# Half-width score tiles, transposed initial states, four-bank spreads and the first groups' sums on VectorE, in a four-layer kernel

## The reference

```python
x = L0(ctx, x, mask)    # attention over concat(ctx, x): 16 heads of 16, 128 keys; RMS norm; gelu MLP; both + x
x = L1(x, state=ctx)    # RWKV-like block; 32 heads of 8; a recurrence over the 64 tokens:
    # s_new = k (x) v + w * s ;  out = r . (faaaa * k (x) v + s) ;  s0 = ctx[:, 2:10]; then a gated channel mix
x = L2(x, ctx, masks)   # causal-style self attention, cross attention to ctx (64 keys each), gelu MLP, layer norms
x = L3(x, ctx, mask)    # x + tanh(gate) * attention of x over layernorm(ctx), 64 keys
```

## Time and profile before

| | |
|---|---|
| median of 3 runs | 1057.02 us (1055.05 to 1059.72) |
| profiled execution, own time | 1057.86 us |
| its span, first to last instruction | 1056.1 us |
| PE busy | 998.5 us (95%) |
| PE weight loads busy | 805.9 us |
| DVE, ACT, POOL busy | 717.6, 599.9, 543.0 us |
| PE's mean granted clock | 0.969 of full |

### The profile page before, as it was taken

The page is one execution under the profiler, slowest core; times in us unless marked ns, Lnnn a source line. Parts: engine busy times, 40 slices in busy tenths (PEclk is TensorE's granted clock), DMA queues, the critical chain, the costliest instruction groups (busy, mean ns, idle before and its releaser), DMA issues.

```text
span 1056.1 us, 27681 instructions
## 1 busy us (share of the span) xinstructions
PE 998.5 (95%) x10976; PEld 805.9 (76%) x10976; DVE 717.6 (68%) x1575; ACT 599.9 (57%) x1460; POOL 543.0 (51%) x666
## 2 busy tenths in 40 slices
PE   7768999989999999999999999999999999999997
PEld 4556877667777778888788877767878778888886
DVE  1224236898899879597553536877899888874765
ACT  2469854324444465546887875227555554675672
POOL 0445325664566655467541436636556774664432
PEclk9958999899999999999999999999999999999999
DMA  9601110001000101001020100100010000000001
GB/s 345 249 2 27 26 25 1 2 2 25 2 2 2 33 2 33 2 24 46 12 58 13 37 2 1 48 1 2 1 27 1 2 13 2 13 2 13 13 2 43
DMA packets 28400, 30.47 MB, mean 29 GB/s; under 512 B 16560, under 2 KB 25072, under 8 KB 27632
## 3 DMA queue, kind: packets, MB, share of 16 engines
q1 hardware_dynamic: 27248, 26.85, 7.9%
q10 hardware_dynamic: 1024, 1.85, 0.5%
HBM read 26.59 MB, written 2.10 MB: 27 GB/s over the span
## 4 chain that ended last, share of the span: by engine, by line
PE 70%; DVE 10%; DVEq 5%; issue 5%; ACT 4%; POOL 3%; ACTq 1%; POOLq 1%; DMA 1%
PE bank L504 10%; PE bank L492 10%; PE bank L366 7%; PE bank L378 7%; PE bank L399 7%; PE bank L391 4%; PE bank L435 3%; PE bank L455 3%; PE bank L479 3%; PE bank L533 3%; PE bank L522 3%; DVE lane L1002 2%; DVEq L1005 2%; DVE bank L998 2%; PE bank L659 2%
## 5 line engine op out<-in xcount | busy, mean ns | idle before, releaser
L1403 POOL TENSOR_TENSOR lane<-lane 128x512 f32<-128x512 f32 x160 | 166.6, 1044 | 210.6 <-DVE lane L881 112.0
L1175 ACT COPY lane<-bank 128x512 f32<-128x512 f32 x232 | 131.3, 586 | 158.3 <-PE bank L366 91.7
L366 PE MATMUL bank<-ident,lane 128*128 128x128 f32 x896 | 136.0, 286 | 15.0 <-ACTq L1238 4.5
L366 PEld LDWEIGHTS bank<-ident,lane 128*128 128x128 f32 x896 | 105.8, 146 | 39.1 <-issue 14.9
L1472 POOL TENSOR_TENSOR lane<-lane 128x512 f32<-128x512 f32 x64 | 81.2, 1269 | 67.3 <-DVE lane L1002 66.9
L1236 ACT ACTIVATE lane<-bank,lane 128x128 f32<-128x128 f32 x256 | 90.7, 372 | 22.3 <-DVE lane L931 21.8
L879 DVE TENSOR_REDUCE lane<-lane 128x8 f32<-128x512 f32 x96 | 65.0, 677 | 30.1 <-ACT lane L1194 29.5
L1002 DVE TENSOR_TENSOR_SCAN lane<-lane,bank 128x256 f32<-128x256 f32 x128 | 80.9, 674 | 5.0 <-issue 0.4
L1143 ACT ACTIVATE lane<-lane 128x256 f32<-128x256 f32 x96 | 52.4, 594 | 49.9 <-POOL lane L1388 49.2
L1157 ACT ACTIVATE lane<-bank,vecs 128x256 f32<-128x256 f32 x112 | 55.7, 552 | 42.4 <-PE bank L366 42.1
L1194 ACT ACTIVATE lane<-lane 128x512 f32<-128x512 f32 x96 | 60.3, 634 | 19.7 <-DVE lane L861 19.4
(11 more groups left out here) (159 smaller groups left out, 2298.3 us busy)
## 6 DMA issues: line engine op xcount, KB each, us to landing
lane<-in_inT SPq DMA_DIRECT2D x16, 256.0 KB, 4.7
lane<-in_x SPq DMA_DIRECT2D x16, 256.0 KB, 2.9
w_d<-in_w_d SPq DMA_DIRECT2D x1, 3072.0 KB, 23.1
w_am<-in_w_am SPq DMA_DIRECT2D x1, 2048.0 KB, 14.8
lane<-in_inT SPq DMA_DIRECT2D x16, 128.0 KB, 2.9
lane<-in_ctx SPq DMA_DIRECT2D x8, 256.0 KB, 3.2
out_x<-lane SPq DMA_DIRECT2D x8, 256.0 KB, 2.2
w_c<-in_w_c SPq DMA_DIRECT2D x1, 1792.0 KB, 14.4
```

Of the source, the lines that this page charges most:

```text
L366: ins = pe.transpose(t[:, i * P:(i + 1) * P], src, ident[:, :])
L1175: s.copy(out, src).then_inc(bk.free_sem(key), 1)
L1403: p.tensor_tensor(q, q, den.unsqueeze(2).to_broadcast([P, n, 512 // n]), ALU.mult).then_inc(sig["normal"].sem, 1)
```

## The change

Five things change, and with them the tables of the order:

1. Scores of the 64-key attentions: the weights of a matmul are now 64 queries of one sequence (32 rows by 64 columns), and the doubled operand is the key (`A.keo`, 128 streamed columns). Two column tiles i (the two sequence pairs) share a bank on different halves of its partitions, so eight tiles can be in work: still 32 matmuls a call. The same two ops on ACT and two on DVE that doubled the queries now double the keys (`v_half`, `s_half`), and the one op that copied the keys now copies the queries. L3's mask matmul becomes 8 of 64 columns each. The cross mask is half as large.
2. The initial states come transposed (`s0T`, 8 rows in each row tile by 256), and enter by four 8-row transposes, one a row tile.
3. `spread_values(m)` fills four banks in one call, 8 matmuls on four row tiles; 16 calls in all.
4. For the first four groups (g < NL) ACT's exponentials no longer sum; DVE sums with a `tensor_reduce`, a drain, and then the reciprocal.
5. `s0T` is 128 KB a group, loaded with the context and cross mask under one semaphore (`bd_loaded`).

```diff
@@ scores
-                        pe.matmul(t[j][:, :].rearrange("p (m k) -> p m k", m=CT), ones_bf[32 * j:32 * j + 1, :],
-                                  L.mask3[32 * j:32 * j + 1, :].unsqueeze(1).to_broadcast([1, CT, T]), start=True, stop=False)
+                    for i in range(TT):
+                        for j in range(PT_):
+                            pe.matmul(t[j][S * i:S * i + S, :].rearrange("p (n k) -> p n k", n=4), ones_bf[32 * j:32 * j + 1, 0:S],
+                                      L.mask3[32 * j:32 * j + 1, P * i:P * i + P].unsqueeze(1).to_broadcast([1, 4, P]), start=True, stop=False)
                 for m in range(CT):
-                    for b in range(G):
+                    for h in range(2):
...
                         for j in range(PT_):
-                            q, at = slice(32 * j, 32 * j + 32), m * T + b * S
-                            ins = pe.matmul(t[j][:, at:at + S], A.qeo[q, m, b, :, :].rearrange("p r q -> p (r q)"),
-                                            A.k[q, m, b * S:(b + 1) * S], start=not masked, stop=not masked or last)
+                            for i in range(TT):
+                                q, b = slice(32 * j, 32 * j + 32), 2 * i + h
+                                o = t[j][S * i:S * i + S, m * T:(m + 1) * T].rearrange("p (r h k) -> p r h k", r=2, h=2)[:, :, h, :]
+                                ins = pe.matmul(o, A.q[q, m, b * S:(b + 1) * S], A.keo[q, m, b, :, :], start=not masked, stop=not masked or last)
@@ spread_values
-            def spread_values(m, i0):
-                t = [pe_open(pe, (g, "spread", m, i)) for i in (i0, i0 + 1)]
+            def spread_values(m):
+                t = [pe_open(pe, (g, "spread", m, i)) for i in range(4)]
                 for e in range(2):
-                    for n in range(2):
-                        q = slice(32 * (i0 + n), 32 * (i0 + n) + 32)
-                        pe.matmul(tokens(t[n][:, e * T:(e + 1) * T])[:, :, 1:S], spread[q, e, :], tokens(L.bv[q, m, :])[:, :, 0:S - 1],
+                    for i in range(4):
+                        q = slice(32 * i, 32 * i + 32)
+                        pe.matmul(tokens(t[i][:, e * T:(e + 1) * T])[:, :, 1:S], spread[q, e, :], tokens(L.bv[q, m, :])[:, :, 0:S - 1],
                                   start=True, stop=True)
-                for n in range(2):
-                    i = i0 + n
-                    pe.matmul(t[n][:, :].rearrange("p (e b t) -> p e b t", e=2, b=G)[:, :, :, 0], ident[:, :], L.s0[:, m, 2 * i:2 * i + 2, :],
-                              start=True, stop=True).then_inc(bk.full_sem((g, "spread", m, i)), 1)
+                for i in range(4):
+                    q = slice(32 * i, 32 * i + 2 * G)
+                    pe.transpose(t[i][:, :].rearrange("p (e t) -> p e t", t=S)[:, :, 0], L.s0T[q, m, :], ident[q, 32 * i:32 * i + 2 * G]).then_inc(
+                        bk.full_sem((g, "spread", m, i)), 1)
@@ v_a
                     v.wait_ge(bk.free_sem((g, "l0", "scores", u)), bk.taken_at((g, "l0", "scores", u)))
+                    if g < NL:
+                        v.tensor_reduce(L.a_den[:, u % 4, :], L.a_probs[:, u % NP_L0, :].rearrange("p (n k) -> p n k", k=P), AX_X, ALU.add)
+                        v.drain()
                     v.reciprocal(L.a_den[:, u % 4, :], L.a_den[:, u % 4, :]).then_inc(sig["den"].sem, 1)
@@ s_a
-                        s.activation(L.a_probs[:, u % NP_L0, i * P:(i + 1) * P], t[:, i * P:(i + 1) * P], ACT.Exp, bias=L.a_nmax[:, u % 4, i:i + 1],
-                                     accum_out=L.a_den[:, u % 4, i:i + 1])
-                    s.drain().then_inc(bk.free_sem(key), 1)
+                        p, src, shift = L.a_probs[:, u % NP_L0, i * P:(i + 1) * P], t[:, i * P:(i + 1) * P], L.a_nmax[:, u % 4, i:i + 1]
+                        if g < NL:
+                            ins = s.activation(p, src, ACT.Exp, bias=shift)
+                        else:
+                            ins = s.activation(p, src, ACT.Exp, bias=shift, accum_out=L.a_den[:, u % 4, i:i + 1])
+                    if g >= NL:
+                        ins = s.drain()
+                    ins.then_inc(bk.free_sem(key), 1)
@@ ORDER and BANKS: all tables are new; the first of PE's lines
-        "P0000011111333332222021200101010011202001002012120101211012213202201201111111111113200201000000212201322202212"
+        "P0000033333111112222210200101201010120220120010120100122113120122000000213301010330002131301210331111011300303"
```

More of the change, by code:

```diff
@@ L379, in pe_cols, with pe_halves @@
             ins.then_inc(bk.full_sem(key), 1)
-        def pe_queries(pe, g, tag, w, x):
+        def pe_halves(pe, g, tag, what, w, x):
             L = lane(g)
@@ L385, in pe_queries @@
             for m in range(CT):
-                key = (g, tag, "q", m)
+                key = (g, tag, what, m)
                 t = pe_open(pe, key)
@@ L446, in weighted @@
                     pe.wait_ge(bk.free_sem((g, tag, "probsT", j)), bk.taken_at((g, tag, "probsT", j)))
-                keys = [(g, tag, "heads", c, i) for i in range(2)]
+                keys = [(g, tag, "heads", c, h) for h in range(2)]
                 t = [pe_open(pe, key) for key in keys]
-                for bp in range(TT):
+                for i in range(TT):
                     for r in range(2):
@@ L692, in pe_b @@
             yield
[L693 to L695 removed]
+            spread_values(1)
             yield
@@ L813, in v_add_rows, with v_half @@
             ins.then_inc(bk.free_sem(key), 1)
-        def v_queries(v, g, tag, qeo, bias, scale):
+        def v_half(v, g, tag, what, out, bias, scale):
             L = lane(g)
             sig = L.sig
-            key = (g, tag, "q", 1)
+            key = (g, tag, what, 1)
             v.wait_ge(bk.full_sem(key), bk.full_at(key))
@@ L1158, in s_normT, with s_half @@
             ins.then_inc(bk.free_sem(key), 1)
-        def s_queries(s, g, tag, qeo, bias, scale):
+        def s_half(s, g, tag, what, out, bias, scale):
             L = lane(g)
             sig = L.sig
-            key = (g, tag, "q", 0)
+            key = (g, tag, what, 0)
             s.wait_ge(bk.full_sem(key), bk.full_at(key))
@@ L1167, in s_queries @@
             for r in range(2):
-                ins = s.activation(qeo[:, 0, :, r, :], src, ACT.Identity, scale=scale[:, r:r + 1],
+                ins = s.activation(out[:, 0, :, r, :], src, ACT.Identity, scale=scale[:, r:r + 1],
                                    bias=qb[:, bias, r:r + 1] if bias is not None else 0.0)
@@ L1343, in s_d @@
             yield
-            key = (g, "l3", "k")
-            s_copy(s, key, flat(L.cross.k), bk.tile(key)[:, :])
+            s_half(s, g, "l3", "k", L.cross.keo, None, par4)
             yield
@@ L1350, in s_d @@
             yield
-            s_queries(s, g, "l3", L.cross.qeo, None, par4)
+            key = (g, "l3", "q")
+            s_copy(s, key, flat(L.cross.q), bk.tile(key)[:, :])
             yield
```

181 lines of the change are left out of this document (88 added, 93 removed).

## The result

| | before, on the same chip | changed kernel |
|---|---|---|
| median | 1058.37 us (4 runs, 1055.05 to 1061.66) | 1042.74 us (4 runs, 1041.88 to 1043.28) |
| ratio | | 0.9852, 95% interval 0.9818 to 0.9886 |
| span of the profiled execution | 1056.1 us | 1041.5 us |
| PE busy / idle in it | 998.5 / 57.6 us | 946.4 / 95.1 us |

What follows compares the result with a forecast made beforehand. The prediction took PE to bound the kernel, with DVE also at its limit in the recurrence stretches. Spreads, scores, sums and give-back summed as 1057.9 - 31 - 23 - 7 + 11 = 1008 us, 1007 on the runs' scale; range 984 to 1036.

Steps and rivals of the forecast that it cites:

- a gain that PE hands over nearly whole: Whole kernel: an edit is worth, to first order, what it takes off PE, busy 998.5 of 1056.1 us.
- the term of 11 us: Recurrence stretches: waiting for four free banks and DVE near its limit give back 11 of the 61 us gained.
- Its bound of 30: Upper bound of the time given back in the recurrence stretches, where the spreads' gains are lost whole; lower bound 0.
- The spreads: Spread of values and initial states: 16 calls of 1.25 us instead of 32 of 1.59, gain 31 us (17 to 32).
- The scores: Scores of the 64-key attentions: a call takes 1.0 us instead of 1.94, 24 calls, gain 23 us.
- Neither end of the bounds: Scores: at worst column tiles don't overlap, 2.0 us a call, nothing won; at best 0.78 us a call, 28 us won.
- The first groups' sums: L0's softmax, 44 to 100 us: ACT's units 0.45 us shorter, gain 7 us, bounds a loss of 6 and a gain of 16.
- The four-bank wait: Rival: PE stops at each of 16 spreads until DVE empties four banks, 4.4 us each, 70 us, 1066 us in all; chance 0.06.
- the column tiles overlap: Scores; the rival said they don't overlap, so scores stay as they are: 1030 us, chance 0.08.
- DVE takes the gain: Rival, recurrence stretches: the spreads' 31 us shorten only PE's busy time, the rest stays: 1028 us, chance 0.20.

Runs made afterwards that it cites:

- experiment 12: Kernel before, its order tables untouched, with the new score tiles and 8-row transposes, sums staying on ACT: 1052.07 us, ratio 0.9952.
- experiment 14: Kernel before with the new score tiles and 8-row transposes, and without DVE's product of values and keys (not computed): 1019.76 us, ratio 0.9624.
- the product left out: DVE's product of values and keys ahead of the scans not computed: 1043.63 us in the kernel before, 1021.54 us in the changed kernel.
- experiment 13: Kernel before without DVE's product of values and keys (not computed): 1043.63 us, ratio 0.9838.
- experiment 1: Changed kernel with the first groups' row sums back on ACT: 1055.2 us, ratio 0.9975.
- experiment 8: Kernel before, with its own order, with only the first groups' row sums moved to DVE: 1059.82 us, ratio 1.0025.
- experiment 7: Changed kernel with the matmuls of each of the 24 score calls issued twice: 1063.51 us, ratio 1.0058.
- experiment 9: Changed kernel with the eight wide matmuls of each spread issued three times: 1060.84 us, ratio 1.0034.
- experiment 10: Changed kernel with the spreads' wide matmuls issued three times and DVE's product of values and keys not computed: 1044.87 us, ratio 0.9877.
- experiment 11: Changed kernel with sums on ACT, score matmuls issued twice and the spreads' wide matmuls three times: 1098.1 us, ratio 1.0378.
- experiment 4: Changed kernel with second halves of the doubled keys of the 64-key attentions moved from DVE to ACT: 1037.66 us, ratio 0.9814.
- experiment 2: Changed kernel with each spread on two row tiles and two banks at a time, in the same place of the order: 1043.0 us, ratio 0.9859.

## Why the prediction was wrong

**The step that failed** is in the first part: "a gain that PE hands over nearly whole", and with it the term of 11 us for what is given back. The measured pair is 52 us less work on PE and 16 us less time, 36 given back; in the old order 41 and 5. PE's 95% busy and its 70% of the chain were read as "PE is the bound, the others have room". They don't say what other way through the program ends how soon. In the old order one of these goes through DVE: taking 41 us off PE brings 5, and taking 43 off DVE as well brings 35 more (experiments 12 and 14). It isn't simply a second chain 5 us shorter than PE's, since then the product left out alone would have brought nothing, and it brought 17 (experiment 13): the ways run through both engines. For the changed kernel itself this isn't shown: with or without the product it gains nearly the same, 16 and 19 us. Why it keeps so little of its 52 us, beyond the waits for DVE and POOL shown above, stays open. The earlier trace rows held the warning, DVE busy 89% and 83% of the recurrence stretches without its drains, and the prediction named it; it then took a fifth of the gain for it, by PE's idle time before, which shows what DVE had cost so far and not what it would cost once PE was faster. With the sizes as measured, 36.5 us of PE's busy time for the spreads, 18.4 for the scores and 7 for the sums, the term would have had to be 62 - 16 = 46 us (43 if the first two are taken as the 52.1 by which PE's busy time fell in all). Its bound of 30 was too low too: it let only the spreads lose their gain.

**The spreads.** The four banks took 2 x 1.59 = 3.18 us in two calls and take 1.08, forecast 1.25; by busy time 58.1 us (L659 and L663) became 21.6. The four row tiles at once are the smallest part of it. Two halves apart take 2 x 1.13 with the 8-row transposes (0.9 us gained), two in a row 1.38 (another 0.9), all four tiles together 1.08 (the last 0.3). Given back to PE in the new kernel, 25.6 us cost 19.

**The scores.** 1.08 to 1.21 us a call (one of 2.01) instead of 1.0, against 1.94 before: 18 us off PE, forecast 23. Neither end of the bounds came true: the two column tiles do run side by side, and at 64 records a call the pace is 17 to 19 ns a record. The statement that matmuls never start closer than about 25 ns (the Trainium skill, "TensorE: Matmul & The Clock Gate", "Wait — 56ns, not 53.3ns?") would make it 1.6 us; the trace has less here too. That counts records, as the prediction did, and a matmul in fp32 is two of them: by matmul, 32 a call, the pace is 34 to 38 ns, and for the values' product 24, which hardly differs from that figure. The clearer case is the 8-row transposes, one record each: four of 169 ns take 0.19 us together, so their starts are about 7 ns apart, an estimate from the row of L665. Whether the gap between two runs of 64 written columns is part of what a call takes above 1.0 us isn't shown; no run has these scores without it.

**The first groups' sums.** The number came out as forecast, 7 us earlier at L0's MLP, and in part by luck. ACT's unit is 0.60 us shorter where 0.45 was taken, and PE's granted clock between 44 and 100 us went from 0.70 to 0.88. But in the new order the sums make 10.8 us (experiment 1), from a start that would be 4 us later than before, and in the old order they make nothing: with them the MLP begins at 104.55 us, against 104.63 (experiment 8). What the part is worth at the end depends on the order: 13 us in the new one, nothing in the old one. There, with the sums on DVE (experiment 8), the stretch from 44 to 100 us has no better clock than before:

```profile
44.00:100.00 56.00, 39.64 (x596) 30.88 (x600) 35.14 (x77) 35.28 (x113) 26.96 (x27) 0.67 0.03 9
```

Whether the sums would pay in the old order once PE is lighter wasn't tried.

**The rivals.** The four-bank wait didn't occur (0.2 us in front of all 16 spreads), and the column tiles overlap. "DVE takes the gain" had the mechanism, limited to the spreads and priced at 20 us. The runs refute the limit: without the sums nearly all of the gain is gone in both orders, that of the scores too. That POOL's or ACT's work holds the end as DVE's does wasn't tested; in the changed kernel PE waits for POOL 14.2 us in the two recurrence stretches. The runs also show that the price isn't a property of the work alone. In the new order time added to PE costs 75 to 100%, in the spreads and in the scores, with DVE's product or without it (experiments 7, 9, 10), and the parts add up (11). In the old order 41 us of PE are worth 5 with the product and 23 without.

**The order.** With the sums put in last, the new kernel's 16 us are 3 us for the lighter PE (5 in the old order) and 13 for the sums, which pay in the new order. With about the old work, the new order is 40 us slower than the old, with the lighter work and the sums on ACT it is 3 us slower, with intervals that overlap. The old order with the lighter work and the sums on DVE wasn't run, so there the two can't be compared. The reading that I find to fit these runs, argued and not shown by itself: each table is fitted to the durations of its own kernel, so that the other engines are just in time beside PE as it then is; the old one has little to give when PE gets faster, and the new one has no room when PE gets slower. Which places of the tables cost the 40 us stays open. The fastest version that computes the whole is experiment 4, which takes 20 us off DVE in the changed kernel.

## What to carry to other kernels

That an engine is 95% busy and has most of the chain is no promise for work removed from it: here 41 us less brought 5, and 52 less, with the sums moved and a new order, 16. Before a rewrite of its matmuls, leave out work of a like size once on that engine and once on the next one, and once on both: the three times say how much of the one gain hangs on the other engine. Where the order is a table, do this in each table that is in question, since the answer differed between the two here. And check in the trace of an experiment that the manipulated engine's busy time has moved by the intended amount, before its verdict is read.

## What the hardware showed that I had not expected

- Four wide matmuls on row tiles 0 and 1, and four on tiles 2 and 3 issued after them, overlap: 1.38 us for both with their transposes, where a whole-array matmul between them made it two times 1.59.
- Four transposes of 8 rows on four row tiles add 0.12 us (172.09 to 172.21), those of two tiles, in experiment 2, 0.12 and 0.10: twice as many cost no more. Why isn't shown.
- ACT loads its tables 61 times in the changed kernel (59 before), mostly at the gelus (L1206) and the exponentials (L1194), 78 us of its 588.7. I hadn't counted them; no run tells what they cost the end. The largest of these groups:

```profile
L1206 ACT ACT_TABLE_LOAD x30 | 38.5, 1283 | 0.9
L1194 ACT ACT_TABLE_LOAD x17 | 21.8, 1283 | 0.3
```
